# All eight value steps of the last attention take their bias on VectorE, and the five engine orders are laid out anew

## The reference

```
x = x + attention0(layernorm(x), ctx)   # 32 query heads on 8 key/value heads, softmax over keys, product with Wo
x = x + ffn0(layernorm(x))              # 512x512 with bias, and a rank-16 LoRA chosen by batch
x = x + attention1(layernorm(x), ctx)   # 16 heads; Q, K and V = x @ W.T + bias; softmax over axis 0
x = x + ffn1(layernorm(x))              # 512x512 with bias, plus a low-rank update through an inverse DFT
```

## Time and profile before

| | before |
|---|---|
| median of three runs | 297.38 us |
| the profiled execution's own time | 297.65 us |
| its span, first to last instruction | 295.9 us |
| PE busy | 290.2 us, 98% |
| PEld busy | 229.8 us, 78% |
| DVE busy | 232.1 us, 78% |
| ACT busy | 162.2 us, 55% |
| POOL busy | 146.9 us, 50% |

### The profile page before, as it was taken

How to read it: one execution, slowest core, us unless ns; L and a number is a source line. 1 busy time by engine, 2 the same in 40 slices (tenths; PEclk the granted TensorE clock), 3 DMA queues, 4 the chain that set the end, 5 groups by cost and what they waited for, 6 DMA issues and landing times.

```text
span 295.9 us, 6338 instructions
## 1 busy us (share of the span) xinstructions
PE 290.2 (98%) x2192; PEld 229.8 (78%) x2192; DVE 232.1 (78%) x374; ACT 162.2 (55%) x276; POOL 146.9 (50%) x193
## 2 busy tenths in 40 slices
...
GB/s 252 351 155 232 112 231 221 107 40 311 31 126 145 142 73 41 0 2 31 139 106 95 52 141 52 125 116 45 128 150 111 210 42 69 2 3 35 73 71 106
DMA packets 32137, 33.10 MB, mean 112 GB/s; under 512 B 3609, under 2 KB 21273, under 8 KB 32107
## 3 DMA queue, kind: packets, MB, share of 16 engines
...
...
## 4 chain that ended last, share of the span: by engine, by line
PE 91%; POOL 4%; DVE 1%; issue 1%; ACT 1%; POOLq 0%; ACTq 0%; DVEq 0%
PE ps L490 18%; PE ps L492 17%; PE ps L491 17%; PE ps L755 5%; PE ps L665 5%; PE ps L835 4%; PE ps L722 3%; PE ps L744 3%; PE ps L763 3%; PE ps L874 3%; PE ps L847 2%; PE ps L772 1%; PE ps L885 1%; PE ps L919 1%; PE ps L678 1%
## 5 line engine op out<-in xcount | busy, mean ns | idle before, releaser
L1225 DVE TENSOR_REDUCE mx<-ps 128x8 f32<-128x1024 f32 x32 | 37.9, 1218 | 4.2 <-PE ps L722 4.0
L1438 POOL TENSOR_SCALAR var_eps<-moments 128x1 f32<-128x1 f32 x32 | 7.1, 222 | 67.9 <-DVE moments L1187 67.0
L1426 POOL TENSOR_TENSOR slot_l<-stg,slot_h 128x512 fp32r<-128x512 f32 x19 | 26.1, 1386 | 21.9 <-ACT slot_h L943 21.9
L490 PE MATMUL ps<-xT_h,slot_h 128*128 128x256 f32 x128 | 36.9, 289 | 0.0
L1022 ACT ACTIVATE PT<-ps 128x1024 f32<-128x1024 f32 x32 | 31.7, 1023 | 8.8 <-PE ps L744 8.7
L492 PE MATMUL ps<-xT_h,slot_l 128*128 128x256 f32 x128 | 36.0, 281 | 0.0
L491 PE MATMUL ps<-xT_l,slot_h 128*128 128x256 f32 x128 | 36.0, 281 | 0.0
L490 PEld LDWEIGHTS ps<-xT_h,slot_h 128*128 128x128 f32 x128 | 24.2, 189 | 2.0 <-issue 0.6
L1468 POOL TENSOR_TENSOR zpart<-P 128x512 f32<-128x512 f32 x16 | 21.3, 1330 | 7.2 <-ACT P L1089 6.3
L491 PEld LDWEIGHTS ps<-xT_l,slot_h 128*128 128x128 f32 x128 | 24.2, 189 | 0.3
L492 PEld LDWEIGHTS ps<-xT_h,slot_l 128*128 128x128 f32 x128 | 24.2, 189 | 0.0
...
## 6 DMA issues: line engine op xcount, KB each, us to landing
...
```

Of the source, the lines that this page charges most:

```text
L490: eng.matmul(dst, left[0], right[0], start=start, stop=False)
L1225: dve.tensor_reduce(mx[:, b % 2, :].rearrange("p (x r) -> p r x", r=REP)[:, r, :], wide(step).rearrange("p k (g t) -> p (k g) t", g=4), AX ...
L1426: pool.tensor_tensor(lo, src, hi.bitcast(F32), ALU.subtract).then_inc(w_lo_pool, 1)
```

## The change

Only the five texts change. `V1.0` to `V1.5` leave `ACT_TEXT` and enter `DVE_TEXT`, so that by L859 to L864 their bias product is gone and by L1359 VectorE adds the bias. All other steps stay on their engines, and all five orders are laid out anew, with new bank numbers. The parts at the start and at the end of the diff, cut to what is spoken of:

```diff
 PE_TEXT = """
-XT.0.1:4 XT.0.0:7 V0.0:0 V0.1:1 Q0.0.0:5 K0.0:0 Q0.0.1:6 MX.0.1:4 MX.0.0:0 V0.2:3 ...
+XT.0.1:3 XT.0.0:1 V0.0:2 V0.1:0 K0.0:6 Q0.0.0:4 Q0.0.1:3 MX.0.0:6 MX.0.1:0 V0.2:2 ...
...
-S1.14:1 S1.15:4 WE.1:6 SM.14:0 V1.7:7 SM.15:0 WE.2:1 WE.0:6 WE.3:2 V1.4:3 V1.5:2 V1.2:1 V1.3:2 PV1.6:3 PV1.7:2
-OX1.6:1 V1.0:3 PV1.4:0 PV1.5:2 OX1.7:0 V1.1:1 XT.3.6:3 OX1.4:2 PV1.3:1 PV1.2:0 OX1.5:2 F1.6:3 OX1.3:1 OX1.2:2
-XT.3.7:0 XT.3.4:3 PV1.1:1 PV1.0:2 F1.7:0 OX1.1:2 OX1.0:1 XT.3.5:3 F1.4:0 ...
+S1.14:2 S1.15:4 WE.2:6 SM.14:0 V1.7:0 SM.15:0 WE.0:2 WE.1:1 WE.3:2 V1.4:1 V1.5:0 V1.2:1 V1.3:3 PV1.6:0 PV1.7:2
+V1.0:3 OX1.6:0 V1.1:2 PV1.4:1 OX1.7:0 PV1.5:1 OX1.4:3 XT.3.6:0 PV1.3:2 PV1.2:1 OX1.3:2 OX1.5:0 F1.6:3 XT.3.4:1
+OX1.2:2 XT.3.7:0 PV1.0:3 PV1.1:2 F1.7:0 OX1.0:3 XT.3.5:2 OX1.1:1 F1.4:0 ...
 ACT_TEXT = """
-SET.8 W.wkv.0 LNn.0.0 W.wkv.1 XT.0.1 XT.0.0 W.wq0.0 W.wq0.1 W.wq0.2 V0.0 W.wq0.3 V0.1 CT.0.2 K0.0 Q0.0.0 ...
+LNn.0.0 W.wkv.0 XT.0.1 W.wkv.1 XT.0.0 W.wq0.0 W.wq0.1 V0.0 V0.1 W.wq0.2 K0.0 W.wq0.3 SET.8 Q0.0.0 ...
...
-K1.15 SM.13 CT.2.4 SM.14 SM.15 FM.3 CT.2.5 W.wbase.3 CT.2.2 EC CT.2.3 FP.3 V1.5 W.wbase.0 W.wbase.2 FP.1 CT.2.0
-W.wbase.1 V1.4 V1.3 V1.2 PV1.6 CT.2.1 PV1.7 PV1.4 V1.0 FP.0 PV1.5 LNn.3.6 V1.1 XT.3.6 ...
+SM.12 K1.14 SM.13 WM CT.2.4 SM.14 SM.15 CT.2.5 W.wbase.2 FM.3 W.wbase.0 EC CT.2.2 FP.3 CT.2.3 FP.1 W.wbase.3 CT.2.0
+CT.2.1 W.wbase.1 PV1.7 FP.0 PV1.6 PV1.4 LNn.3.6 PV1.5 XT.3.6 ...
 DVE_TEXT = """
-K1.14 K1.15 S1.14 S1.15 FM.3 V1.6 WE.1 FE.3 V1.7 WE.2 WE.0 WE.3 CE CL.2.5 FZ.3 FR.3 FF.3 NM.12 FF.1 NM.15 NM.14 FF.2
-NM.10 NM.9 NM.11 NM.8 OX1.6 FF.0 LNs.3.6 NM.5 NM.7 OX1.7 LNs.3.7 NM.6 XT.3.6 OX1.4 LNs.3.4 NM.0 OX1.5 NM.2 F1.6
+FZ.2 FR.2 K1.14 BV S1.14 V1.6 S1.15 FM.3 WE.2 V1.7 FE.3 WE.0 WE.1 CL.2.5 CE WE.3 FZ.3 FR.3 V1.4 FF.3 NM.12 FF.2 V1.5
+NM.15 FF.1 NM.14 V1.3 NM.5 NM.8 FF.0 NM.11 NM.10 V1.2 OX1.6 NM.9 LNs.3.6 NM.6 V1.0 V1.1 OX1.7 NM.7 LNs.3.7 OX1.4
+XT.3.6 LNs.3.4 NM.2 OX1.3 OX1.5 NM.0 F1.6 ...
 POOL_TEXT = """
-SET.1 SET.2 SET.0 LNs.0.0 LNs.0.1 ...
+SET.0 SET.2 SET.1 LNs.0.0 LNs.0.1 ...
...
-L.wbase.2 CL.2.1 LNs.3.6 NM.3 XB.6 L.wbase.1 LNs.3.7 LNs.3.4 NM.1 XB.7 XB.4 LNs.3.2 LNs.3.5 LNs.3.3 XB.5 LNs.3.0
+L.wbase.2 NM.3 L.wbase.3 LNs.3.6 L.wbase.1 NM.1 LNs.3.7 LNs.3.4 XB.6 XB.7 LNs.3.5 LNs.3.3 LNs.3.2 XB.5 XB.4 LNs.3.1
```

More of the change, by code:

```diff
@@ L73 @@
+S1.10:2 K1.13:0 K1.12:1 Q1.14:0 SM.11:0 SM.10:0 Q1.15:5 K1.15:2 S1.12:0 S1.13:3 WM:6 SM.13:0 SM.12:0 K1.14:5 V1.6:7
+S1.14:2 S1.15:4 WE.2:6 SM.14:0 V1.7:0 SM.15:0 WE.0:2 WE.1:1 WE.3:2 V1.4:1 V1.5:0 V1.2:1 V1.3:3 PV1.6:0 PV1.7:2
+V1.0:3 OX1.6:0 V1.1:2 PV1.4:1 OX1.7:0 PV1.5:1 OX1.4:3 XT.3.6:0 PV1.3:2 PV1.2:1 OX1.3:2 OX1.5:0 F1.6:3 XT.3.4:1
+OX1.2:2 XT.3.7:0 PV1.0:3 PV1.1:2 F1.7:0 OX1.0:3 XT.3.5:2 OX1.1:1 F1.4:0 XT.3.2:3 F1.5:1 XT.3.3:2 F1.2:0 XT.3.0:2
+F1.3:3 XT.3.1:2 F1.0:0 FH.1.1:1 FH.1.0:3
 """
```

119 lines of the change are left out of this document (58 added, 61 removed).

## The result

The kernel after takes 303.16 us (median of four runs, 301.98 to 303.30) against 297.35 us for the kernel before beside it: ratio 1.0185, interval 1.0155 to 1.0214. It is 5.8 us slower. The forecast was 300.0 us with 301.4 as its upper end, so the direction was right and the size was not. Measured again later on another chip (c0), the kernel gave 302.69 us, ratio 1.0161 (1.0145 to 1.0177).

The account below looks back on a forecast made before the run. TensorE, busy 98% of the span, was taken as the bound, with VectorE close to late at 239 to 262 us. 297.65 + 1.2 (late) + 1.4 (start) + 0 (middle) = 300.25 profiled, 300.0 us as median; range 297.0 to 301.4.

Parts of the forecast that it names:

- The start: Kernel's first steps: later idle products and K0.0's wait, less swallowed gaps, cost +1.4 us (bounds 0 and +2.4).
- The clears: At the start, GpSimd clears KS before V0, so idle products begin 1.8 us later and V0.0 1.1 us later.
- K0.0's wait: At the start, K0.0 directly behind V0.1 waits 0.85 us for ScalarE's copy (bounds 0 and 1.2).
- Rival 1: At the start, the clock rises at the same moment as before; V0.0 only 0.4 us later; 299.3 us, chance 0.16.
- The middle: From 45 to 228 us, new orders with about the same distances and the same DMA transfers: 0 (-1.0 to +1.0).
- The late part: Last layer: TensorE's won products against new waits on VectorE, +1.2 us (bounds -1.4 and +2.2).
- F1.6 starts at 265.4: Late part: after VectorE's read of XT.3.6 and 0.4 us of transposes, F1.6 starts 1.6 us later than 263.80.
- A product less on TensorE is time won at once.: TensorE has few gaps, so dropping six products wins 1.37 us unless something is late behind it.
- rival 2: Late part: VectorE's cover holds and nothing waits, -1.4 cancels the start's +1.4; 297.4 us, chance 0.15.
- the small faster case: Below 296.5 us, chance 0.14, mostly the new order closing TensorE's gaps in the first 237 us (295.8 us, chance 0.13).
- Rival 5: Late part: TensorE had room, so the six products are worth 0 and the waits stay; 301.4 us, chance 0.02.
- Rival 4: More new waits, in the middle or in the last batches; 301.8 us, chance 0.09.

Follow-up runs that it names:

- c5: The kernel before with only GpSimd's three clears put in the order of after; 298.61 us, ratio 1.0030.
- d5: The kernel after with clears and ScalarE's start as before, L.wv1.1 early, ScalarE's and GpSimd's late orders repaired, K0.0 still ahead; 302.44 us, ratio 1.0148.
- d2: The kernel after with all five late orders as in before from V1.6 on, V1.0 to V1.5 on ScalarE with bias products; 300.88 us, ratio 1.0092.
- c1: The kernel after with L.wv1.1 alone put back ahead of Q1.13 in VectorE's order; 301.94 us, ratio 1.0134.
- b2: The kernel before with the six bias products of V1.0 to V1.5 left out and nothing in their place; 297.55 us, ratio 0.9990.
- b1: The kernel before with only V1.0 to V1.5 moved from ScalarE to VectorE and their six bias products dropped; 301.18 us, ratio 1.0117.
- a5: The kernel after with V1.0 to V1.5 copied by ScalarE again, bias products on TensorE, other orders kept; 302.50 us, ratio 1.0167.

## Why the prediction was wrong

1. **The start, forecast +1.4: measured +1.56 (0.81 + 0.75).** The sum is right partly by luck. The clears were put at +1.1 and cost 0.7 to 0.9 (c5; 0.81 in this pair). K0.0's wait was put at 0.85; counted the same way it is 0.7, 0.55 more than before's own. And the 0.5 us that I took off, because TensorE's early gaps would be swallowed, did not come: the rest of the way to K0.1 is 0.2 us longer instead. That K0.0 waits no longer in after is due to ScalarE's weight pieces, which had been moved out of its way; where they were not, the profile lists 1.65 us of idle time at it (0.70 + 0.95 in d5), against 0.19 in after. Rival 1, a clock that rises at the same moment, is refuted by the idle products: every one of the eleven kernels with the late first product still has them 0.85 us apart between 5.63 and 6.48 us, when TensorE in before was already fast. The Trainium skill, page TensorE: Matmul & The Clock Gate, Part 1, says that the monitor runs freely and does not start anew with a kernel. The spread of the rise among these eleven agrees with that; that the rise would keep its moment when the first product moves was my own conclusion, and the traces are against it.

2. **The middle, forecast 0 (-1.0 to +1.0): measured +2.1 in the profiled execution, +1.3 on average.** This is the step that failed. It rested on "the DMA queue has the same transfers; the weights of the last layer are asked for in the order in which they are now used". The transfers are the same; what the runs showed in its place is a load that its user waits for, WM 2.0 us longer than 1.87. I had not checked what lets each load be issued: the gathers in front of it on SP, and the staging slot that VectorE empties. These parts stood in the diff: LW.dft.3 went behind the gathers QX.13 and QX.12, LW.dft.1 behind LW.dft.2, and L.wv1.1 behind K1.12. They took the lead of LW.dft.1 on its product from 4.6 to 3.9 us. The other half no list shows: with that lead the load came in time in one kernel of nine (d2, 3.1 us to landing) and late in eight (3.9 to 5.45 us), though the two loads ahead of it always took 2.9 to 3.1. Why the last one is slow is open. That the place of L.wv1.1 matters is shown by c1 and the five other kernels that have it early, none of which waits over 0.04 us at WM; LW.dft.1 ahead of LW.dft.2 was not tried alone. With the mean of 202.0 us from K0.1 to V1.6 in the five kernels with the middle of before, the nine with after's have 203.35 (201.8 to 204.6), and the difference follows WM's wait. Without WM's excess over 1.87 us the nine have 202.1 on average: the rest of the new middle is as good as the old one. That part of the zero was right.

3. **The late part, forecast +1.2 (-1.4 to +2.2): measured +1.98, steady to 0.1 us in seven kernels that kept these orders.** Counted from V1.6, VectorE's XT.3.6 was forecast 2.45 us later and came 2.49 later, without idle time from FZ.3 on. Two errors cancel in this: FZ.3 was to come 0.8 earlier and came 0.16 earlier (14.27 to 14.11 us behind V1.6; VectorE's own steps CE and WE.3 stand ahead of it, not GpSimd's sum), and the way from there took 24.3 us in place of 24.9. The mis-sized step is the next: "F1.6 starts at 265.4", 1.1 us behind VectorE's read. It is 1.75 behind (268.01 to 269.76), since XT.3.6 on TensorE had itself waited for the normed row, through ScalarE's and GpSimd's lists, and two PV1 and two OX1 steps had still to follow. I had followed one list by hand, and the step hangs on three.

4. **"A product less on TensorE is time won at once."** b2 shows 0.33 of 1.38 us. The sum did not use the full 1.4 as a gain, since F1.6 went by VectorE, but the bound of -1.4, rival 2 and the small faster case did: with nothing at all put on VectorE the late part was -0.3. Rival 5 said the products are worth nothing, after the Trainium skill's page Trainium Kernel Development and Optimization, section Performance Expectations, which calls the matmuls' busy time a bad metric. b2 comes near its result (0.33 us, not 0), though not by room on TensorE: products start 0.23 us apart without gaps in both traces. By the waits that b2's trace lists it is ScalarE and GpSimd that are due just behind.

5. **Rival 4, more new waits, at 301.8 with a chance of 0.09,** is the one that came true in kind, in the middle as it said, and on top of the late ones; its time is 1.4 us short of the measured one. It deserved more: the five texts hold over a thousand steps, all laid out anew, and I gave the part without rows the narrowest bounds.

6. **The change alone.** In the orders of before it costs 4.1 us in the late part (b1), in orders laid out for it 2.0 (after), and inside those it is worth nothing either way (a5). So the 2.0 us belong to the late orders as they stand (d2 brings them back), with or without the change: the new orders took away what the change costs in the old ones and cost 2.0 us themselves.
